# A sampling layer and a 7x7 involution in one program section, on one core of a Trainium2 chip

## What is computed

```python
x = x + _L0_conv_ref(_gn(x), ...)      # deformable sampling, 3x3 depthwise
x = x + _L1_conv_ref(_gn(x), ...)      # involution, 7x7
x = x + _L2_conv_ref(_gn(x), ...)      # deformable sampling with a mask, 3x3
x = x + _L3_conv_ref(_gn(x), ...)      # attention, 8 heads

# L1: 49 weights for each channel and pixel, from a reduced map of 32 channels
    h = relu(batchnorm(w1 @ x + b1))
    wgt = (w2 @ h + b2).reshape(B, C, 7, 7, H, W)
    for i in range(7):
        for j in range(7):
            out = out + wgt[:, :, i, j] * xp[:, :, i:i + H, j:j + W]

# L2: 27 maps from a 3x3 convolution: 18 offsets and 9 masks
    om = _conv(x, w_om, b_om)
    sampled = bilinear samples of x at 9 displaced points per pixel, times sigmoid(mask)
    out = einsum('bckhw,ock->bohw', sampled, w_dc) + b_dc
```

## Time and profile before

| what | us |
|---|---|
| median of 3 runs | 2243.61 (2240.99 to 2244.31) |
| the profiled execution, own time | 2243.17 |
| its span, first to last instruction | 2241.3 |
| first sampling section ends, about | 466.9 |
| first and last row sum of the involution start | 491.2, 826.2 |
| second sampling section | 831 to 1086.7 |
| attention section | 1086.7 to 2241.3 |

### The profile page before, as it was taken

How to read it: one execution, slowest core, us unless ns; L and a number is a source line. 1 busy time by engine, 2 the same in 40 slices (tenths; PEclk the granted TensorE clock), 3 DMA queues, 4 the chain that set the end, 5 groups by cost and what they waited for, 6 DMA issues and landing times.

```text
span 2241.3 us, 36271 instructions
## 1 busy us (share of the span) xinstructions
PE 1775.6 (79%) x12208; PEld 1003.2 (45%) x12208; DVE 1751.3 (78%) x4342; ACT 1136.6 (51%) x2902; POOL 1146.7 (51%) x1269
## 2 busy tenths in 40 slices
PE   4444444468888876444599999999999999999998
PEld 2444444435454543444435555555534444444433
DVE  5777777769999985777598888887888888888871
ACT  3333333320000003333448888888777777777776
POOL 3777777726666664777587777777231000000000
PEclk8667666669999998666779999999999999999999
DMA  7666666600000006666443433343001111111101
GB/s 248 206 206 206 205 206 206 205 16 1 1 1 1 1 5 201 205 206 208 102 126 100 115 107 105 105 114 107 14 9 28 28 23 24 26 23 20 22 1 43
DMA packets 90664, 211.60 MB, mean 94 GB/s; under 512 B 18544, under 2 KB 43760, under 8 KB 90352
## 3 DMA queue, kind: packets, MB, share of 16 engines
q0 software_dynamic: 51840, 169.91, 25.3%
q1 hardware_dynamic: 38640, 39.38, 8.0%
HBM read 174.62 MB, written 13.37 MB: 84 GB/s over the span
## 4 chain that ended last, share of the span: by engine, by line
PE 42%; ACT 4%; issue 2%; DVE 2%; POOL 1%; DMA 0%; SPq 0%; ACTq 0%; POOLq 0%
PE ps L1385 13%; PE ps L1349 13%; PE ps L1363 11%; ACT l_e L1095 3%; PE ps L1442 2%; PE ps L1432 1%; PE ps L1370 1%; DVE l_mx L1219 1%; ACT corner L1066 1%; PE ps L1396 1%; POOL l_part L963 0%; PE ps L1402 0%; POOL corner L953 0%; PE ps L1423 0%; PE ps L1409 0%
## 5 line engine op out<-in xcount | busy, mean ns | idle before, releaser
L1219 DVE TENSOR_REDUCE l_mx<-ps 128x1 f32<-128x384 f32 x1728 | 835.6, 549 | 129.7 <-PE ps L1363 129.6
L1095 ACT ACTIVATE l_e<-ps 128x384 f32<-128x384 f32 x1728 | 726.1, 511 | 217.4 <-PE ps L1349 215.5
L1363 PE MATMUL ps<-l_ka,l_qs 96*128 96x384 bf16 x1728 | 572.0, 334 | 13.9 <-DMA l_qs<-l_part 9.4
L1349 PE MATMUL ps<-l_qs,l_ks 99*128 99x384 bf16 x1728 | 565.3, 330 | 10.3 <-ACT l_e L1095 4.6
L253 POOL DMA_INDIRECT l_corner<-table,l_idx x324 | 315.4, 973 | 129.2 <-issue 98.1
L418 DVE SCALAR_TENSOR_TENSOR l_samp<-l_corner,l_wts,l_samp 128x128 f32<-128x128 f32 x972 | 284.9, 348 | 111.4 <-ACT l_samp L336 103.7
L1385 PE MATMUL ps<-l_e,l_v_s 128*32 128x384 f32 x3456 | 331.2, 491 | 1.6 <-ACT l_e L1095 0.8
L649 DVE SCALAR_TENSOR_TENSOR l_prod<-ps,c_b,l_pad 128x384 f32<-128x384 f32 x588 | 312.3, 609 | 25.0 <-PE ps L684 25.0
L1349 PEld LDWEIGHTS ps<-l_qs,l_ks 99*128 99x128 bf16 x1728 | 166.3, 97 | 365.0 <-ACT l_e L1095 192.9
L512 PE MATMUL ps<-l_turned,l_wk 128*128 128x128 f32 x648 | 146.2, 419 | 213.0 <-ACT l_turned L344 213.0
L585 POOL TENSOR_TENSOR l_prod<-l_prod 128x1152 f32<-128x1152 f32 x84 | 221.3, 2635 | 140.6 <-DVE l_prod L649 140.6
(11 more groups left out here) (169 smaller groups left out, 1894.9 us busy)
## 6 DMA issues: line engine op xcount, KB each, us to landing
table<-l_tok SPq DMA_DIRECT2D x16, 640.0 KB, 6.6
l_ka<-l_part SPq DMA_DIRECT2D x96, 72.0 KB
l_ks<-l_part SPq DMA_DIRECT2D x96, 72.0 KB
l_corner<-table,l_idx POOLq DMA_INDIRECT x324, 3.7
l_qs<-l_part SPq DMA_DIRECT2D x96, 48.0 KB, 2.1
corner<-table,idx POOLq DMA_INDIRECT x270, 3.6
l_qs<-l_part SPq DMA_DIRECT2D x96, 24.0 KB
out<-x_map SPq DMA_DIRECT2D x12, 192.0 KB, 1.9
```

Source lines behind the costliest of these rows:

```text
L1095: nc.scalar.activation(e[:, w % 2, i, :], ps[:, st_bank(at), 0:QC], ACT.Exp).then_inc(s["st_free"], 1)
L1219: nc.vector.tensor_reduce(mx[:, ga % MAX_SLOTS, u // NQC, u % NQC:u % NQC + 1], ps[:, ab_bank(at), 0:CH], AX.X, ALU.max) \
L1349: nc.tensor.matmul(ps[:, bank, 0:QC], ks[:, head % 2, kt * 128:(kt + 1) * 128], qs[:, gb % 3, j * QC:(j + 1) * QC], start=True, stop=True) \
L1363: nc.tensor.matmul(ps[:, bank, 0:CH], qs[0:KROWS, ga // CT % 3, q0:q0 + 128], ka[:, head % 2, k0:k0 + CH], start=True, stop=True).then_inc ...
```

## The change

`involution_layer` and `sampling_layer(True)` become one section, `middle_layer`. It runs over 97 steps. Steps 0 to 83 are the involution's rows. A step of an engine holds its involution work and, at fixed places, work of the second sampling:

- Steps 46 to 54 prepare batch 0, whose part of x is finished at step 45: statistics chunk by chunk, group norm, table, offsets, indices. Steps 88 to 96 prepare batch 1 in the same way. In batch 0 all of PE's side results go through one PSUM bank, 6.
- Tile i of batch 0 takes the two steps 58 + 2i and 59 + 2i on PE (three groups of nine transposes, then nine matmuls), so that 13 of the 18 tiles lie beside rows 58 to 83. POOL fetches a tile's nine gathers in steps 55 + 2i and 56 + 2i, into two slots instead of three.
- A tile's work is divided in another way: ACT scales corners 0, 2 and 3 (27 instructions, L680), DVE mixes in corner 1 alone (9 instructions, L836), PE adds the three parts by accumulating transposes (27 instead of 9, L999), and ACT takes out one group of three taps at a time from the one bank.
- The weight maps are made in trios of taps into a ring of six banks (`TRIO`, `W_RING`) instead of 4 and 3 into seven.
- Rows 56, 58, ... 82 (14 rows) get no sum on POOL: PE accumulates all seven products, 21 transposes instead of 12 (`unsummed`, `streams`).
- DVE computes the indices before the four corner weights, and group norm statistics of layer 2 are taken by chunks as the involution goes.

```diff
+TRIO, W_RING, SIDE, ACC = 3, 6, 6, 7
+NORM2_AT = (NCH * K7 + LAG + 1, B * NCH * K7 + LAG + 1)
+GATHER_AT = NORM2_AT[0] + 12
+STEPS = GATHER_AT + 2 * TILES + 3
...
+        def unsummed(row):
+            return row >= GATHER_AT - 3 and (row - GATHER_AT) % 2 == 0
+        def streams(row):
+            return K7 if unsummed(row) else NA
...
+                def fetch(i, gr):
...
+                    if i >= 2:
+                        pool.wait_ge(s["turned_mm"], (i - 2) * GROUPS + gr + 1)
+                    for k in range(gr * GK, (gr + 1) * GK):
+                        nc.gpsimd.indirect_dma_start(
+                            corner[:, i % 2, k, :], None, from_row[0],
...
+                for step in range(STEPS):
+                    beat = step - GATHER_AT
...
+                    if beat >= -3:
+                        if beat % 2:
+                            fetch((beat + 3) // 2, 0)
+                            fetch((beat + 3) // 2, 1)
+                        else:
+                            fetch((beat + 2) // 2, 2)
+                            if step - 1 < ALL_ROWS:
+                                sum_row(step - 1)
+                    elif step < ALL_ROWS:
+                        sum_row(step)
...
+                    if beat % 2 == 0:
+                        scale_corners(tile + 1, 0, 6)
+                        take_turned(tile, 0)
+                        scale_corners(tile + 1, 6, 13)
+                    else:
+                        scale_corners(tile + 1, 13, 18)
+                        take_turned(tile, 2)
+                        scale_corners(tile + 1, 18, 27)
...
+                    if beat % 2 == 0:
+                        if j == 0:
+                            add_sample(tile - 1)
+                        if j == 1:
+                            mix(tile, 2)
+                        if j == 5:
+                            mix(tile + 1, 0)
+                    else:
+                        if j == 3:
+                            mix(tile + 1, 1)
+                        if j == 4:
+                            sample_stats(tile - 1)
...
-                    if row:
-                        pe.wait_ge(s["products"], (row - 1) * K7 + taps[-1] + 1)
+                    if n >= 2:
+                        pe.wait_ge(s["products"], TRIO * (n - 1))
...
+                    pe.wait_ge(s["products"], (row + 1) * K7)
+                    if not unsummed(row):
+                        pe.wait_ge(s["psum"], sum(not unsummed(r) for r in range(row + 1)))
...
+                for step in range(STEPS):
+                    q = step - LAG
+                    trios = range(K7 * step // TRIO, K7 * (step + 1) // TRIO) if step < ALL_ROWS else ()
+                    for n in trios[:1]:
+                        weights(n)
+                    if 0 < q <= ALL_ROWS and q % K7 == 1:
+                        add(q - 1, range(streams(q - 1)))
+                    if 0 < q < ALL_ROWS and q % K7:
+                        add(q, range(1))
+                    side(step, 0)
+                    for n in trios[1:]:
+                        weights(n)
+                    if 0 < q < ALL_ROWS and q % K7:
+                        add(q, range(1, streams(q)))
...
-            sampling_layer(nc, g, False)
-            involution_layer(nc, g)
-        sampling_layer(nc, g, True)
+            sampling_layer(nc, g)
+            middle_layer(nc, g)
```

569 lines of the change are left out of this document (403 added, 166 removed).

## The result

| | us |
|---|---|
| before, median of 4 runs | 2242.70 (2240.99 to 2244.31) |
| after, median of 4 runs | 2202.32 (2200.95 to 2204.62) |
| ratio | 0.9821, 95% interval 0.9804 to 0.9838 |
| forecast | 2167, range 2152 to 2200 |

What follows compares the result with a forecast made beforehand. DVE bounds the involution and POOL's issuing the sampling. First gather 734.5 + beside rows 210.8 + last tiles 34.2 + tail 30.7 = 1010.2 instead of 1086.7, 76.5 us less: 2167 us, range 2152 to 2200.

Steps and rivals of the forecast that it cites:

- The trios: Weight maps in trios cost nothing, between a gain of 10 us and a loss of 5 (0.1 us a row).
- Rival 3: The double buffer of trios takes the waits at chunk ends away: 2157 us, chance 0.09.
- The preparation: Batch 0's preparation beside rows, steps 46 to 54, delays the first gather by 19 us.
- The last offsets and the index chain: Before the first gather: of 6.2 us before, the new order puts about 3.9 us ahead of the indices.
- Beside rows: Steps 55 to 84: POOL's nine gathers and one sum set 14.05 us a tile, 15 of them 210.8 us.
- Rival 1: PE sets the pace beside rows, 15.5 to 16.8 us a tile: 2179 to 2198 us, chance 0.22.
- Rival 2: DVE's mixes and POOL's sums exclude each other, at most 0.9 us a tile for POOL: 2180 us, chance 0.07.
- Rivals 4 and 5: Clock falls, slower than before, 2260 us, chance 0.04; overlap doesn't come off, near no change, 2240 us, chance 0.03.
- After the last sum: Behind POOL's step 84: three tiles left at 11.4 us, 34.2 us, then 30.7 us to the section's end.
- The tail: Last gather's landing, scales, transposes, copies and batch 1's offset convolution to indices, to the section's end: 30.7 us.
- Attention: The attention section is the same code and was left at 1154.6 us.
- The last warning of the forecast: Wrong if DVE, PE and ACT wait in turn around bank 6, whose loop had 3.6 us to spare.

Runs made afterwards that it cites:

- a2: Kernel before with only the weight maps made in trios into a ring of six banks, nothing of the second sampling moved: 2265.58 us.
- a1: Changed kernel with PE making two trios of weight maps, not one, before the transposes at a chunk's first step: 2184.55 us.
- c4: b2 with seven of the nine taps of batch 0's offset convolution left out, so batch 0 samples other places: 2170.32 us.
- b2: a1 with layer 2's chunk statistics on DVE behind the product of tap 3 instead of tap 6: 2178.62 us.
- c2: b2 with PE doing a tile's combination (18 matmul instructions) behind the next row's first trio, not ahead of it: 2172.34 us.
- b4: a1 with PE transposing only the first of three parts of each batch 0 sample, the others left out of the result: 2186.36 us.
- a4: Changed kernel with DVE's mix of a tile's third group behind the product of tap 3 instead of tap 1: 2199.73 us.
- d3: c2 with a tile's third mix two products later, away from POOL's sum: 2174.90 us.
- c5: b2 with DVE adding a tile's sample directly before the first product of the weight maps behind the tile's combination: 2178.13 us.
- d2: c2 with DVE's norm of batch 0 split into two halves with three products between them: 2171.79 us.

## Why the prediction was wrong, point by point

- **The trios, costed at nothing between a gain of 10 and a loss of 5.** This step failed. Up to row 45's sum the rows took 189.3 us from the first sum, where before took 181.9. Of these 7.4 us 2.4 are the statistics as forecast, and by subtraction 5.0 the trios, just inside the bound. But the value taken was zero, a2 shows 20.6 for all 84 rows, and a1 gets back 17.8 in the changed kernel. "PE's turn at a chunk end stays as it was" was the wrong sentence: the transposes stayed, and DVE's products in hand beside them fell from four to one. Rival 3, which had the double buffer gain there, has the wrong sign.
- **The preparation, 19 us.** It took 64.9 - 36.75 = 28.1, 9.1 more. c4 confirms the offset convolution's price and that it lies bare. The 9.1 are, by reading: 1.7 for L776 behind the sum; 4.2 of DVE waiting for bursts at half clock; and 3.2 at the chunk start in row 53 (10.92 us in after, 7.73 in a1 and b2 with two trios first; 1.0 of it is the burst of fifteen, 2.85 us for 1.83). b2 shows the first with a part of the second (row 47, 4.4 us), a1 the third; the second was not isolated. The first sum of after starts 1.8 us earlier than that of before, which hides as much of the loss.
- **The last offsets and the index chain, 3.9 us.** They took 6.2. Their cast (L811) had to wait for a sum and took 2.63 us, where the next cast took 0.33.
- **Beside rows, 14.05 us a tile with POOL as the bound.** This step failed too: 210.8 forecast, 224.9 measured, 211.3 in c2. What was put at nothing is the waiting of PE and DVE for each other. The sums for DVE (11.0 us) and PE (13.4 to 14.8) counted work in two rows. They did not lay out in what pieces it lies between two trios. PE has 4.2 us of foreign work where DVE has 1.6 us of products, and two rows took 15.8 us, more than POOL's 13.8 and than PE's upper figure. DVE's lead, forecast at some 11 us when the sum of row 57 comes up, was 8.9, and 0.9 was left of it at row 63. In c2 two rows take 14.7 us, and the lead nearly lasts. That c2 then meets the forecast's 210.8 is in part luck: a gather costs POOL 1.25 us and not 1.27, so fifteen of its own periods are 207 us, and some 4 us are waits that the forecast had at nothing.
- **Rival 1, PE sets the pace (0.22; 2179 to 2198).** Nearest to what happened, and its range ends 4 us short. Its signature came true, POOL waiting for products and transposes and periods of 15 us or more. Its pace of 15.5 to 16.8 us a tile holds the measured 15.8, and it named the trade at every trio. That PE's amount of work at 88% busy sets this pace did not hold: c2 gained 6 us with all of it there, PE being busy for 194.8 of 210 us (93%). b4 fits that, but its clock fell, so it weighs less.
- **Rival 2, exclusion of mixes and sums (0.07).** It occurs and costs DVE alone, 1.3 us a tile where there is room (a4, d3). The forecast was right to price the mixes at nothing. It looked for the exclusion at the mixes only, and the two places where it cost something are small operations on the way to the first gather, L776 and L811. The Trainium skill, "SBUF — State Buffer", section "Who interferes with whom", says that copies, casts and tensor-scalar operations can also take the pair of ports that GpSimd shares, when their operands meet certain conditions. By that rule L811 and the norm can have to wait for a sum too, and the trace agrees: 2.63 against 0.33 us, and 2.17 against 0.87.
- **Rivals 4 and 5.** The clock was 0.94 in the stage, far from the 0.70 that rival 4 needs (though PE was busy for 86% of it, not for over 90), and the overlap came off. The forecast had no term for short falls of the clock, and they came: the clock is 0.91, 0.90 and 0.91 in the periods of 18.7, 16.6 and 19.3 us, in the first of them at the chunk start.
- **After the last sum.** Three tiles 35.0 for 34.2. The tail took 2.0 more: a tile's combination (18 matmul instructions, 2.27 us at 1022.83) stands on PE inside batch 1's offset convolution, and the forecast had left it out of the list. Attention took 2.1 more, and no run says why.

The last warning of the forecast, engines that wait in turn for one another, was the right one. It named bank 6 as the place, and the loop through bank 6 was not it: c5 took PE's waits there away and gained nothing.

The fastest versions that compute all of the layer are c2 and d2, 2172.34 and 2171.79 us, which can't be told apart. c2 is 70 us below before and 30 below the changed kernel. Its terms are near the forecast's, after two moves that the forecast did not have: first gather 732.8 for 734.5, stage 211.3 for 210.8, end of the section at 1011.8 for 1010.2.

## What to carry to other kernels

Where two engines hand over in small pieces, write down what stands between two handovers and what the other has in hand meanwhile, at the worst place of the loop; work per period and busy shares don't show it. A finer handover is no gain in itself: it moves the handover against the long bursts, and what counts there is how many products the other engine has in hand. A pause of the matrix engine there can cost twice, when its clock falls for the burst behind it. When work is laid beside a long operation of another engine, look at the smallest operations of the critical chain too, since each may have to wait for the rest of the long one.
